# A graph layer with routed experts on one core: accumulating transfers listed by a new rule, in two batches, and node groups of two tiles at the end

## The chip, the core and the metric

The kernel is one program on one core of a Trainium2 chip. The metric is the device time of one execution in microseconds; a kernel's figure is the median of its runs. PE is the matrix engine, DVE the vector engine, ACT the scalar engine, POOL the GpSimd engine; SP only starts DMAs. Each engine works through its own instruction list in order and waits at semaphores.

## What is computed

```python
def reference(x, src, dst, ...):          # x: 6250 nodes x 256, 106250 edges
    x = x + relu(segment_sum(norm_src * (layernorm(x) @ W)[src], dst) * norm_dst + b)
    n = layernorm(x)                      # then a feed-forward of 8 experts
    top_p, top_idx = top_k(softmax(n @ Wr + br), 2)
    w = top_p / top_p.sum(-1)             # of 2 experts per node
    y_e = gelu(expert_norm_e(n) @ W1[e] + b1[e]) @ W2[e] + b2[e]   # 256 -> 1024 -> 256
    return x + w[0] * y_{e0} + w[1] * y_{e1}
```

Every node gathers the rows of its in-neighbours; then each node's row goes through two of eight experts, and both results are weighted and added to the node's row.

## The kernel before, in words

**Edges.** The edges are sorted by target and cut into 832 tiles of 128. A step `fetch` gathers 128 source rows by an indirect DMA of POOL (L832) into a ring of 23 buffers `gt`; a step `tile` multiplies them on PE with a one-hot matrix `S` (L1165). After eight tiles, `add` (L1534) adds the sum to `acc`, which holds all 49 node tiles of 128 nodes.

**Nodes.** The 49 node tiles form eight chunks (ending at tiles 10, 17, 24, 31, 36, 41, 45, 49), and each chunk is cut into groups of at most four tiles. When the last edge of a group is added, a group has these steps: `nd1` (degree norm, DVE), per tile `nT`, `nW`, `hh`, `xT`, `lg` (transpose, W, residual and statistics, transpose, router logits; PE, ACT, DVE), `nd2` (layernorm factors; for tiles from 10 on SP then stores the rows of `acc` to `out`), `lr` (logits) and `xr` (normed rows into `xrow`).

**Routing.** When a chunk's groups are done: `r1` (top 2), `r3` (counts by matmul on PE, L1222 and on), `r5` (slots `slI`, DVE, L1451), `xs` (two indirect DMAs of POOL per node tile scatter the rows to `xs` in DRAM, sorted by expert, L861), `r6` (which expert each block of 256 rows has, DVE). For the last chunk SP also writes eight blank blocks (`blanks`, L1002).

**Blocks.** 56 blocks of 256 routed rows; chunk 6 gives blocks 34 to 37, chunk 7 gives 38 to 55. For each block SP loads rows and weights (`ld`: L1024 rows, L1028 `w1b` 1 MB; `ld2`: L1034 `w2b` 1 MB). PE does `turn` (transpose, L1235), four `up` (L1251) and two `down` (L1266); ACT the gelu; DVE `low`, `split` and `y` (L1688). A block's first `up` needs its `low`; `down` needs its four `split`. The hidden tiles `h32` rotate through four buffers.

**Putting results together.** Blocks 0 to 33 are early: SP stores their results to `ys` (L991), and once all edge tiles are done a step `cg` per node tile (0 to 40) gathers two rows per node from there on POOL (L880), and `cc` (DVE, L1699 to L1706) weights and adds them into `acc`. The gathered rows rotate through ten buffers, so `cg` t waits for `cc` t-10. Tiles 0 to 9 are complete then and SP stores them to `out` (L987). Tiles 10 to 40 were stored before without their expert results; their `cc` makes the sum alone, and `sums` adds it to `out` by one accumulating DMA per batch of tiles (L900). Blocks 34 to 55 are late: their results are added straight to `out` by a `give`, two accumulating indirect DMAs (L891). Gives and batches may hit the same rows, so each waits on POOL until the one before has landed; the first also waits for all plain stores to `out` (`wait_last`). Late results rotate through three buffers `yb` and then eight in `gt`.

**What sets the order.** A planner (`plan`, run when the program is built) simulates clocks of the four engines with costs in us and writes one list of steps; each engine gets the steps that concern it in that order. The steps of DMAs started by SP come in the same list. `step_give` decides when a give or a batch may be listed: not before `s["chain"]` (the supposed landing of the one before) and not when POOL's clock is too far ahead. `step_job` lists steps of nodes, routing and gathers. `free` ignores POOL.

Of the kernel before, what the change touches and what calls it, by code (L numbers as in the profile page):

```python
# [6 lines left out]
N, D, E, H = 6250, 256, 8, 1024  # L7
# [19 lines left out]
ENDS = [10, 17, 24, 31, 36, 41, 45, 49]  # L27
STEP = 4
CHUNKS = list(zip([0] + ENDS, ENDS))
PARTS_OF = [-(-(t1 - t0) // STEP) for t0, t1 in CHUNKS]  # L30
GROUPS = [(c, t0 + (t1 - t0) * i // k, t0 + (t1 - t0) * (i + 1) // k)
# [30 lines left out]
TG = CHUNKS[EARLY][1]  # L62

TP = 10
NSUM = -(-(TG - TP) // 11)
SUMS = [(TP + (TG - TP) * i // NSUM, TP + (TG - TP) * (i + 1) // NSUM) for i in range(NSUM)]
NA = NB - M0
# [99 lines left out]
def plan():  # L167

    order = []
    clock = {"PE": 0.0, "DVE": 0.0, "ACT": 0.0, "POOL": 0.0}  # L170
# [8 lines left out]
    def emit(kind, arg, costs, ready):  # L179
        order.append((kind, arg))  # L180
        t = ready
        for eng, us in costs:
            t = max(t, clock[eng]) + us
            clock[eng] = t
            t += 0.2
        return t + HAND
# [102 lines left out]
    gives = collections.deque()  # L289

    batches = collections.deque()

    def step_give():

        if max(s["chain"], s["plain"], s["base"]) > s["now"] or clock["POOL"] > s["now"] + 2.6:
            return False
        if batches and batches[0][0] <= s["now"]:
            b = batches.popleft()[1]
            emit("sums", b, (("POOL", 1.3 * (SUMS[b][1] - SUMS[b][0])),), s["now"])
            s["summed"] += 1  # L300
        elif gives:
            emit("give", gives.popleft(), (("POOL", 3.4),), s["now"])
            s["given"] += 1
        else:
            return False
        s["chain"] = clock["POOL"] + 5.0
        return True
# [32 lines left out]
    def step_job(front):  # L340
# [4 lines left out]
        for job in list(itertools.islice(front, 2 if front is jobs or front is sends else 1)):  # L345
            job.over()
            for chain in job.heads():
                if not chain.steps:
                    continue
                kind, arg, costs = chain.steps[0]  # L350
                if chain.at > s["now"] or not free(costs):
                    continue
                if kind == "cg" and clock["POOL"] > s["now"] + 2.5:
                    continue
# [49 lines left out]
                if kind == "routed":  # L404
                    s["routed"] = arg
                chain.at = end + 2.0 if kind == "cg" else s["now"] if kind == "xs" else end
                job.at = max(job.at, end)
# [51 lines left out]
def gnn_ffn(nc, x, src, dst, W, b, Wr, br, ln_g, ln_b, W1, b1, W2, b2, out):  # L459
# [8 lines left out]
    with ctx:  # L468
# [61 lines left out]

        PW, PL, PR, PV = PS[7][:, 0:256], PS[7][:, 256:256 + STEP * E], PS[7][:, 288:384], PS[7][:, 384:512]

# [1204 lines left out]
```

How the kernel before makes its waits and increments, by code:

```python
        def pool(e):  # L747
            def made(inst):
                inst.then_inc(s_const, 1)
            def count(tile, pattern, base=0, mult=0):
                made(e.iota(tile, pattern=pattern, base=base, channel_multiplier=mult, allow_small_or_imprecise_dtypes=True))
            made(e.memset(ident[:, :], 0.0))
            e.wait_ge(s_const, const["ident0"])
            made(e.affine_select(out=ident[:, :], in_=ident[:, :], compare_op=ALU.not_equal,
                                 fill=1.0, base=0, pattern=[[-1, 128]], channel_multiplier=1))
            count(irep[:, :, :], [[1, 128], [0, TC]])
            made(e.memset(ones[:, :], 1.0))
            made(e.memset(oneb[:, :], 1.0))
            e.wait_ge(s_const, const["oneb"])
            made(e.affine_select(out=tri[:, :], in_=oneb[:, :], compare_op=ALU.is_gt,
                                 fill=0.0, base=0, pattern=[[1, 128]], channel_multiplier=-1))
            count(irun[:, :, :], [[1, 128], [0, CT]])
            count(area[:, :], [[AREA, E]])
            count(room[:, :], [[AREA * BS, E]])
            count(gone[:, :], [[AREA, E]])
            count(rev[:, :], [[-1, E]], base=E)
            count(kio[:, :], [[1, MB]])
            count(pio[:, :], [[0, 1]], mult=1)
            e.wait_ge(s_const, const["pio"])
            for g in range(NGR - 1):
                inst = e.tensor_scalar(tardy[:, g:g + 1], pio[0:R, :], float(AFTER[g]), None, ALU.is_ge)
                if g == NGR - 2:
```

## Time and profile before

| | |
|---|---|
| median of 3 runs | 1668.92 us |
| the runs | 1669.75, 1660.30, 1668.92 us |
| profiled execution, its time | 1661.44 us |
| profiled execution, its span | 1660.0 us |
| mean granted PE clock | 0.82 |
| PE, POOL, DVE, ACT busy | 1192.6, 1116.0, 952.5, 595.0 us |
| chain that ended last: PE, DMA, POOL | 35%, 25%, 19% of the span |
| fetches (L832) on POOL | 832 of 1.0 us, 133 to 1338 us of the span |
| gives (L891) on POOL | 44 issues, 1394.7 to 1652.7 us |

A span runs from the first to the last instruction; the time of the execution holds what lies around it too. The chain is followed back from the last instruction to what released it. In the rows of a timeline the bracket at the end is how long the engine stood before this instruction and what ended that; in the rows of the chain of waits there is a start, a duration and what was under way, and a DMA there is the stretch from issue to landing.

### The profile page before, as it was taken

What the parts mean: (1) busy time and instruction counts of PE and PEld (TensorE: products, weight loads), DVE (VectorE), ACT (ScalarE), POOL (GpSimd) and SP (SyncE); (2) the same over time, 40 slices, a digit from 0 to 9 for tenths busy, and PEclk for the clock granted to TensorE, in tenths of its full rate; (3) what the DMA queues carried; (4) which work ended last, traced back from release to release, by engine and by line L of the source; (5) the groups of instructions that cost most, each with busy time, mean ns of one, the idle gap of its engine ahead of it and who ended that gap; (6) DMA issues with size and microseconds to landing.
All of it is one profiled execution on the core that took longest, in us unless ns stands there. A gap on an engine that the chain in (4) does not pass through costs nothing.

```text
span 1660.0 us, 26618 instructions
## 1 busy us (share of the span) xinstructions
PE 1192.6 (72%) x9098; PEld 989.6 (60%) x9098; DVE 952.5 (57%) x2502; ACT 595.0 (36%) x1169; POOL 1116.0 (67%) x1115
## 2 busy tenths in 40 slices
PE   6954565647358645995599659969839858689995
PEld 5954344535146314982488439848728747479984
DVE  8997456656434353656264734764645749466552
ACT  4954011111032004440345025516315335356662
POOL 5006777777777777777777777777777757673333
PEclk9999566666578557996699769979959969799998
DMA  6027866675375447974787469759658578999882
GB/s 187 1 98 266 266 219 203 213 232 179 117 260 163 110 119 261 312 222 129 260 270 253 138 217 316 255 192 305 188 189 292 179 252 265 258 294 305 264 251 51
DMA packets 195546, 354.75 MB, mean 214 GB/s; under 512 B 25572, under 2 KB 93446, under 8 KB 195412
## 3 DMA queue, kind: packets, MB, share of 16 engines
q1 hardware_dynamic: 130120, 205.39, 36.6%
q0 software_dynamic: 58928, 141.26, 29.5%
q10 hardware_dynamic: 6364, 6.40, 1.2%
q8 instruction: 73, 1.20, 0.3%
q14 instruction: 61, 0.50, 0.1%
HBM read 290.80 MB, written 64.07 MB: 214 GB/s over the span
## 4 chain that ended last, share of the span: by engine, by line
PE 35%; DMA 25%; POOL 19%; issue 9%; DVE 8%; ACT 3%; SPq 0%; POOLq 0%; DVEq 0%; ACTq 0%
DMA gt<-zt,srcI 12%; POOL gt L832 9%; PE ps L1251 9%; PE ps L1266 9%; PE ps L1165 8%; DMA out<-gt,toks 6%; POOL xs L861 6%; DMA out<-acc 3%; PE ps L1140 2%; POOL out L891 2%; PE ps L1176 2%; DVE ohl L1340 2%; PE ps L1203 2%; DMA xb<-xs 1%; ACT h L1112 1%
## 5 line engine op out<-in xcount | busy, mean ns | idle before, releaser
L832 POOL DMA_INDIRECT gt<-zt,srcI x832 | 834.1, 1003 | 254.2 <-issue 181.6
L1165 PE MATMUL ps<-gt,S 128*128 128x257 f16 x1664 | 345.7, 331 | 200.3 <-DMA gt<-zt,srcI 198.9
L1165 PEld LDWEIGHTS ps<-gt,S 128*128 128x128 f16 x1664 | 203.5, 152 | 298.2 <-DMA gt<-zt,srcI 282.8
L1251 PE MATMUL ps<-xe,w1b 128*128 128x256 f16 x2688 | 343.2, 282 | 36.0 <-DVE xe L1656 18.9
L1266 PE MATMUL ps<-w2b,hT 128*128 128x256 f16 x2688 | 315.5, 275 | 13.5 <-DVE yb L1688 7.7
L1251 PEld LDWEIGHTS ps<-xe,w1b 128*128 128x128 f16 x2688 | 269.9, 101 | 78.6 <-DVE xe L1656 21.6
L1112 ACT ACTIVATE h<-ps,cb 128x256 f32<-128x256 f32 x448 | 227.1, 557 | 241.4 <-PE ps L1251 236.4
L1662 DVE SCALAR_TENSOR_TENSOR hT<-h,cb,hT 128x512 f16<-128x512 f32 x224 | 167.7, 750 | 237.4 <-ACT hT L1116 236.8
L1266 PEld LDWEIGHTS ps<-w2b,hT 128*128 128x128 f16 x2688 | 264.3, 99 | 47.5 <-issue 15.4
L1116 ACT ACTIVATE hT<-h,cb 128x512 f16<-128x512 f32 x224 | 161.7, 722 | 7.3
L1090 ACT ACTIVATE aT<-ps 128x256 f32<-128x256 f32 x98 | 37.4, 381 | 314.7 <-PE ps L1196 314.6
L1388 DVE TENSOR_TENSOR S<-dlo,S 128x1024 f16<-128x1024 f16 x104 | 71.6, 689 | 102.4 <-PE ps L1165 101.7
L891 POOL DMA_INDIRECT out<-gt,toks x38 | 60.1, 1581 | 92.9 <-DMA out<-gt,toks 64.4
L1100 ACT ACTIVATE xe<-ps 128x512 f16<-128x512 f32 x56 | 32.5, 580 | 244.6 <-PE ps L1235 244.6
L861 POOL DMA_INDIRECT xs<-xrow,slI x98 | 98.4, 1004 | 29.9 <-issue 29.9
L1235 PE MATMUL ps<-ident,xb 128*128 128x128 f32 x224 | 37.9, 296 | 104.0 <-DMA xb<-xs 104.0
L1656 DVE SCALAR_TENSOR_TENSOR xe<-ps,xe 128x512 f16<-128x512 f32 x56 | 38.3, 683 | 120.5 <-ACT xe L1100 120.5
L1534 DVE SCALAR_TENSOR_TENSOR acc<-ps,dhi,acc 128x257 f32 x208 | 91.1, 479 | 22.8 <-PE ps L1165 8.8
L1235 PEld LDWEIGHTS ps<-ident,xb 128*128 128x128 f32 x224 | 28.3, 152 | 107.5 <-DMA xb<-xs 106.7
L1140 PE MATMUL ps<-ohh,ohl 128*128 128x49 bf16 x832 | 84.3, 278 | 9.7 <-DVE ohh L1341 8.9
L1140 PEld LDWEIGHTS ps<-ohh,ohl 128*128 128x128 bf16 x832 | 81.5, 150 | 12.8 <-DVE ohh L1341 12.8
L1176 PE MATMUL ps<-gb,w1b 128*128 128x1 f32 x256 | 52.4, 339 | 34.5 <-DMA w1b<-in_L_ffn_W 34.5
(264 smaller groups left out, 1246.7 us busy)
## 6 DMA issues: line engine op xcount, KB each, us to landing
w1b<-ws SPq DMA_DIRECT2D x56, 1024.0 KB, 6.5
w2b<-ws SPq DMA_DIRECT2D x56, 1024.0 KB, 8.1
ws<-w2b SPq DMA_DIRECT2D x16, 1024.0 KB, 5.0
xb<-xs SPq DMA_DIRECT2D x56, 260.0 KB, 8.3
gt<-zt,srcI POOLq DMA_INDIRECT x832, 4.2
ys<-yb SPq DMA_DIRECT2D x34, 256.0 KB, 7.8
w1b<-in_L_ffn_W SPq DMA_DIRECT2D x8, 1024.0 KB, 8.7
hT<-in_L_ffn_W SPq DMA_DIRECT2D x8, 1024.0 KB, 13.9
```

The source lines that it names most:

```text
L832: e.indirect_dma_start(out=gt[:, i % NG, :], out_offset=None, in_=zt, in_offset=bass.IndirectOffsetOnAxis(ap=srcI[:, c, r:r + 1].bitcast(u ...
L861: e.indirect_dma_start(out=xs, out_offset=bass.IndirectOffsetOnAxis(ap=slI[:, i, CHUNKS[c][0] + j:CHUNKS[c][0] + j + 1].bitcast(u32), axis=0),
L891: e.indirect_dma_start(out=out, out_offset=bass.IndirectOffsetOnAxis(ap=toks[:, a, i:i + 1].bitcast(u32), axis=0), in_=late_rows(a)[:, i, ...
L1112: inst = e.activation(h32[n % NH][:, z, :], UP[n % 2][:, z * BS:(z + 1) * BS], ACT.Gelu, bias=cb[m % 3][:, 2 * q + z:2 * q + z + 1], scale ...
L1116: e.activation(hT[m % 2][:, 0, 2 * q:2 * q + 2, :], h32[n % NH][:, :, :], ACT.Copy, scale=cb[m % 3][:, 9:10]).then_inc(s_hi, 1)
L1140: inst = e.matmul(PS[6][:, 0:T], ohl[c % 2][:, :, j], ohh[c % 2][:, :, j], start=(c == 0 and j == 0), stop=(c == NCH - 1 and j == TC - 1))
L1165: inst = e.matmul(PS[r % 2][:, 0:257], S[:, r % NS, :, c], gt[:, i % NG, part * 257:part * 257 + 257], start=(c == 0 and part == 0), stop= ...
L1176: inst = e.matmul(PV[:, j:j + 1], w3[:, kk, j * 128:(j + 1) * 128], gb[:, ex, 2 + kk:3 + kk], start=(kk == 0), stop=(kk == 1))
L1251: inst = e.matmul(UP[n % 2][:, z * BS:(z + 1) * BS], w[:, l, kk, j * 128:(j + 1) * 128], xe[m % 2][:, k, kk, :], start=(kk == 0 and l == 0 ...
L1266: inst = e.matmul(PY[:, h * D:(h + 1) * D], hT[m % 2][:, k, j, h * 128:(h + 1) * 128], w[:, l, j, :], start=(j == 0 and l == 0 and k == 0) ...
L1534: inst = e.scalar_tensor_tensor(out=a, in0=PS[r % 2][:, 0:257], scalar=dhi[:, w, r:r + 1], in1=a, op0=ALU.mult, op1=ALU.add)
L1662: e.scalar_tensor_tensor(out=hT[m % 2][:, 1, 2 * q:2 * q + 2, :], in0=h32[n % NH][:, :, :], scalar=cb[m % 3][:, 9:10], in1=hT[m % 2][:, 0, ...
```

## The change

It has four parts. (1) The last two chunks (tiles 41 to 48) are cut into groups of two tiles in place of four. (2) The sums of tiles 10 to 40 go to `out` in two batches (15 and 16 tiles) in place of three (10, 10, 11). (3) The planner's rule for gives and batches: they are listed only when POOL's clock is at most 0.5 us ahead (was 2.6 us), a give is taken as 3.7 us of POOL and landed 4.5 us later (was 3.4 and 5.0), a batch as 2.0 us of POOL and landed 3.0 + 1.1 us per tile later (was 1.3 us per tile of POOL and 5.0). (4) Gathers and scatters are listed only when POOL's clock is at most 0.3 us ahead, and not when the chain of gives comes free within about 1 us; a gather counts as landed 6.0 us after (was 2.0).

```diff
 ENDS = [10, 17, 24, 31, 36, 41, 45, 49]
-STEP = 4
 CHUNKS = list(zip([0] + ENDS, ENDS))
-PARTS_OF = [-(-(t1 - t0) // STEP) for t0, t1 in CHUNKS]
+
+STEPS = [4] * (len(ENDS) - 2) + [2, 2]
+PARTS_OF = [-(-(t1 - t0) // step) for (t0, t1), step in zip(CHUNKS, STEPS)]
...
-NSUM = -(-(TG - TP) // 11)
+NSUM = 2
...
-        if max(s["chain"], s["plain"], s["base"]) > s["now"] or clock["POOL"] > s["now"] + 2.6:
+        if max(s["chain"], s["plain"], s["base"]) > s["now"] or clock["POOL"] > s["now"] + 0.5:
             return False
         if batches and batches[0][0] <= s["now"]:
             b = batches.popleft()[1]
-            emit("sums", b, (("POOL", 1.3 * (SUMS[b][1] - SUMS[b][0])),), s["now"])
+            emit("sums", b, (("POOL", 2.0),), s["now"])
+            s["chain"] = clock["POOL"] + 3.0 + 1.1 * (SUMS[b][1] - SUMS[b][0])
             s["summed"] += 1
         elif gives:
-            emit("give", gives.popleft(), (("POOL", 3.4),), s["now"])
+            emit("give", gives.popleft(), (("POOL", 3.7),), s["now"])
+            s["chain"] = clock["POOL"] + 4.5
             s["given"] += 1
         else:
             return False
-        s["chain"] = clock["POOL"] + 5.0
         return True
...
-                if kind == "cg" and clock["POOL"] > s["now"] + 2.5:
+                if kind in ("cg", "xs") and (clock["POOL"] > s["now"] + 0.3 or (gives or batches) and s["now"] + 1.0 < max(s["chain"], s["plain"], s["base"]) + 1.0 < s["now"] + 2.0):
                     continue
...
-                chain.at = end + 2.0 if kind == "cg" else s["now"] if kind == "xs" else end
+                chain.at = end + 6.0 if kind == "cg" else s["now"] if kind == "xs" else end
```

POOL's list behind the gather of tile 13, before. `xrow`, `S` and `gt` are the buffers of a gather (two issues each), `xs` is the scatter of chunk 7, L891 a give, L900 a batch:

```order
L880 DMA gt<-ys,cidx 128x256 x6
L891 DMA out<-yb,toks 6250x256 x2
L880 DMA xrow<-ys,cidx 128x256 x6
L861 DMA xs<-xrow,slI 53504x260 x8
L891 DMA out<-yb,toks 6250x256 x2
L880 DMA S<-ys,cidx 128x256 x6
L900 DMA out<-acc 128x10x256
L880 DMA S<-ys,cidx 128x256 x2
L880 DMA gt<-ys,cidx 128x256 x4
L891 DMA out<-yb,toks 6250x256 x2
```

The same place now (lines are two higher):

```order
L882 DMA gt<-ys,cidx 128x256 x4
L863 DMA xs<-xrow,slI 53504x260 x8
L882 DMA gt<-ys,cidx 128x256 x2
L882 DMA xrow<-ys,cidx 128x256 x4
L893 DMA out<-yb,toks 6250x256 x2
L882 DMA xrow<-ys,cidx 128x256 x2
L882 DMA S<-ys,cidx 128x256 x2
L893 DMA out<-yb,toks 6250x256 x2
L882 DMA S<-ys,cidx 128x256 x4
L893 DMA out<-yb,toks 6250x256 x2
```

The scatter stood behind 17 gathers, a give and three more gathers; it stands behind 16 gathers now. From there on two gathers stand between gives, up to the give of block 38; the first batch (15 tiles) follows two gathers later, and the second one stands behind the give of block 42. POOL's whole order of the tail was: give 34, 35, batch 0, 36, 37, 38, batch 1, 39, 40, batch 2, 41 to 55; it is give 34 to 38, batch 0, 39 to 42, batch 1, 43 to 55.

SP's list behind the eight blank blocks, before (loads of blocks 38 and 39; the stores of tiles 7 to 9 stood ahead of the blank blocks):

```order
L1024 DMA xb<-xs 128x2x260
L1028 ISA
L1028 DMA w1b<-ws 128x4x1024
L1034 DMA w2b<-ws 128x4x1024
L1038 ISA
L1038 DMA b2b<-in_L_ffn_b 128x256
L1024 ISA
L1024 DMA xb<-xs 128x2x260
L1028 ISA
L1028 DMA w1b<-ws 128x4x1024
```

and now:

```order
L989 DMA out<-acc 128x256 x2
L1026 ISA
L1026 DMA xb<-xs 128x2x260
L1030 ISA
L1030 DMA w1b<-ws 128x4x1024
L1036 DMA w2b<-ws 128x4x1024
L1040 ISA
L1040 DMA b2b<-in_L_ffn_b 128x256
...
L1030 DMA w1b<-ws 128x4x1024
L989 DMA out<-acc 128x256
```

The stores of tiles 7 and 8 stand ahead of block 38's load, that of tile 9 behind block 39's.

DVE's list at the first blocks of chunk 7, before. L1705 and L1706 are one combining step, `xe` is a `low`, `hT` a `split`; the first combining step here is that of tile 21:

```order
L1652 COPY cb2<-cbt 128x12
L1705 TENSOR_SCALAR acc<-S,wts 128x256
L1706 SCALAR_TENSOR_TENSOR acc<-S,wts,acc 128x256
L1656 SCALAR_TENSOR_TENSOR xe0<-ps5,xe0 128x512
L1705 TENSOR_SCALAR acc<-S,wts 128x256
L1706 SCALAR_TENSOR_TENSOR acc<-S,wts,acc 128x256
L1648 TENSOR_LOAD ek7
L1648 ISA x2
L1652 ISA
L1652 COPY cb0<-cbt 128x12
L1662 SCALAR_TENSOR_TENSOR hT0<-h320,cb2,hT0 128x512
L1662 SCALAR_TENSOR_TENSOR hT0<-h321,cb2,hT0 128x512
```

and now, from the first `split` of block 38 on; the first combining step here is that of tile 19:

```order
L1664 SCALAR_TENSOR_TENSOR hT0<-h320,cb2,hT0 128x512
L1664 SCALAR_TENSOR_TENSOR hT0<-h321,cb2,hT0 128x512
L1707 TENSOR_SCALAR acc<-xrow,wts 128x256
L1708 SCALAR_TENSOR_TENSOR acc<-xrow,wts,acc 128x256
L1664 SCALAR_TENSOR_TENSOR hT0<-h322,cb2,hT0 128x512
L1658 SCALAR_TENSOR_TENSOR xe1<-ps5,xe1 128x512
L1707 TENSOR_SCALAR acc<-S,wts 128x256
L1708 SCALAR_TENSOR_TENSOR acc<-S,wts,acc 128x256
L1664 SCALAR_TENSOR_TENSOR hT0<-h323,cb2,hT0 128x512
L1664 SCALAR_TENSOR_TENSOR hT1<-h320,cb0,hT1 128x512
```

Where the combining steps of tiles 21 and 22 stood around the `low` of block 38, that of tile 19 now stands between two `split` steps of block 38 and ahead of the `low` of block 39.

## Rows read from the trace of the kernel before

**Rows 1.** The page: busy time, share of the span, instructions, by engine.

```profile
PE 1192.6 (72%) x9098; PEld 989.6 (60%) x9098; DVE 952.5 (57%) x2502; ACT 595.0 (36%) x1169; POOL 1116.0 (67%) x1115
```

**Rows 2.** Windows: stretch, length, busy per engine, PE clock, DMA share, GB/s.

```profile
1444.00:1480.00 36.00, 34.32 (x313) 30.35 (x311) 20.89 (x50) 23.68 (x43) 28.50 (x24) 1.00 1.02 326
...
1534.00:1600.00 66.00, 66.00 (x607) 59.40 (x606) 34.09 (x79) 43.86 (x81) 24.75 (x16) 1.00 0.85 258
```

**Rows 3.** Chain of waits, 1200 to 1660 us: start, duration, what.

```profile
1384.37 9.38 DMA out<-acc
...
1428.55 14.97 DMA out<-acc
...
1480.22 12.14 DMA out<-acc
...
1506.73 8.72 DMA out<-gt,toks
...
1516.30 17.46 DMA out<-acc
...
1536.67 6.71 DMA out<-gt,toks
```

**Rows 4.** Timeline of POOL: start, duration, instruction, idle before.

```profile
1348.94 0.94 POOL L880 DMA_INDIRECT S<-ys,cidx  x1 [11.19 <-DMA ys<-yb]
1350.19 0.95 POOL L880 DMA_INDIRECT S<-ys,cidx  x1 [0.30 <-issue]
...
1394.66 1.62 POOL L891 DMA_INDIRECT out<-yb,toks  x1 [1.94 <-DMA out<-acc]
...
1406.31 1.17 POOL L861 DMA_INDIRECT xs<-xrow,slI  x1 [0.31 <-issue]
...
1444.49 1.63 POOL L891 DMA_INDIRECT out<-yb,toks  x1 [6.45 <-DMA out<-acc]
...
1534.60 1.78 POOL L891 DMA_INDIRECT out<-gt,toks  x1 [16.30 <-DMA out<-acc]
...
1631.70 1.56 POOL L891 DMA_INDIRECT out<-gt,toks  x1 [5.67 <-DMA out<-gt,toks]
...
1638.28 1.56 POOL L891 DMA_INDIRECT out<-gt,toks  x1 [3.15 <-DMA out<-gt,toks]
...
1643.74 1.55 POOL L891 DMA_INDIRECT out<-gt,toks  x1 [2.04 <-DVE gt L1694]
...
1649.29 1.55 POOL L891 DMA_INDIRECT out<-gt,toks  x1 [2.14 <-DMA out<-gt,toks]
```

**Rows 5.** Timeline of PE.

```profile
1344.13 0.65 PE L1165 MATMUL ps<-gt,S 128*128 128x257 f16 x2 [2.18 <-DMA gt<-zt,srcI]
...
1389.84 0.24 PE L1222 MATMUL ps<-Mb,oneb 128*128 128x8 bf16 x4
...
1422.21 1.12 PE L1235 MATMUL ps<-ident,xb 128*128 128x128 f32 x4 [5.43 <-DMA xb<-xs]
...
1442.60 2.58 PE L1251 MATMUL ps<-xe,w1b 128*128 128x256 f16 x22 [1.55 <-DVE xe L1656]
```

**Rows 6.** Timeline of DVE.

```profile
1397.13 0.52 DVE L1451 CAST slI<-slF 128x8 int32<-128x8 f32 x1
...
1407.72 0.75 DVE L1688 SCALAR_TENSOR_TENSOR yb<-ps,cb,b2b 128x512 f32<-128x512 f32 x1
...
1429.22 0.55 DVE L1705 TENSOR_SCALAR acc<-S,wts 128x256 f32<-128x256 f32 x1 [10.70 <-DMA S<-ys,cidx]
...
1642.35 0.62 DVE L1694 TENSOR_SCALAR gt<-gt,gate 128x256 f32<-128x256 f32 x2
```

**Rows 7.** Timeline of SP: DMAs that it starts.

```profile
1397.22 9.60 SPq L1002 DMA_DIRECT2D xs<-blank  x8
...
1418.68 0.40 SPq L1024 DMA_DIRECT2D xb<-xs  x1
...
1623.97 0.37 SPq L1034 DMA_DIRECT2D w2b<-ws  x1
```

More of the change, by code:

```diff
@@ L529, in gnn_ffn @@
         PY, PX, PA = PS[4], PS[5], PS[6]
-        PW, PL, PR, PV = PS[7][:, 0:256], PS[7][:, 256:256 + STEP * E], PS[7][:, 288:384], PS[7][:, 384:512]
+        PW, PL, PR, PV = PS[7][:, 0:256], PS[7][:, 256:256 + max(STEPS) * E], PS[7][:, 288:384], PS[7][:, 384:512]
         ph = ExitStack()
```

## The prediction

> **What bounds the kernel now.** I read the page's sums first: PE is busy for 72% of the span, POOL for 67%, DVE for 57% [rows 1]. No engine is full, so the order of work decides, and the place of the change has to be read. The lists of steps are alike through most of the gathers of edges: PE's and DVE's up to chunk 6's first node group, POOL's up to ten fetches before chunk 6's scatter. So I went to the windows of the tail [rows 2]: from 1444 to 1480 and from 1534 to 1600 us the DMA engines' share is 1.02 and 0.85, and PE is busy 34.3 of 36 us and 66.0 of 66 us.
>
> The chain of waits from 1500 on [rows 3] is one alternation: a give (two indirect accumulating DMAs into `out`, L891), its landing, the next give. Gives 41 and 52 start at 1534.60 and 1631.70 [rows 4], 11 periods of 8.83 us. Three batches (L900) stand in the same chain with 14.97, 12.14 and 17.46 us of transfer [rows 3], about 0.95 us more until the next give begins (1444.49 - 1428.55 - 14.97) [rows 3, 4]. The last give starts at 1649.29, 10.7 us before the span's end. The other bound is near: the last block's `y` ends at 1642.97 (1642.35 + 0.62) [rows 6], so PE and DVE have only 6.3 us to spare.
>
> If the chain had been tight from its first give at 1394.66, 18 periods of 8.83, three of the short ones at the end (6.6, 5.5, 5.5) and 47.4 for the batches would have ended at 1618: it has some 31 us of slack. The slack lies between 1394 and 1534, where three gather steps (2.5 us each, two issues, one every 1.25 [rows 4]), a scatter of 8 issues and PE's late blocks stand between gives. Block 38, the first of the last 18, waits for the last chunk's routing: `r3` at 1389.84 [rows 5], slots at 1397.65 [rows 6], the scatter only at 1406.31 because POOL had a give and three gather steps first [rows 4], the load at 1418.68 [rows 7], its turn at 1422.21 [rows 5].
>
> **The change, term by term.**
> 1. *Groups of two tiles.* Two more nd1, nd2 and lr steps are small DVE work beside fetches. What counts is what PE does between the last tile (its matmuls end at 1344.8) and `r3` of chunk 7, so far 45.0 us [rows 5]. Four `up` steps (12 matmuls each, 66.0 us / 607 [rows 2], 1.31 us), one turn and two tiles' node work leave this stretch: about 10 us of busy work, plus part of its waits, as block 34 now runs under the last fetches. I take 13 us earlier, 1377, between 10 (only the busy work) and 16. Slots follow `r3` by 7.8 us: 1385.
> 2. *Scatter.* It moves in front of gather 16 and of all gives, so it starts with its slots, 21 us earlier, and ends near 1395.5. The load of block 38 also stands behind eight blank stores (9.60 us from 1397.22, `r3` + 7.4 [rows 7]) and behind the stores of tiles 7 and 8. These need `y` of block 36, which began at `r3` + 17.9 [rows 6]: all three conditions meet at `r3` + 21 to 22, so 1399. Block 38 begins 20 us earlier.
> 3. *What the first give waits for.* It needs the stores of tiles 0 to 9 landed. Tile 9's used to be issued before the blanks; now it stands on SP behind five loads of blocks 38 and 39, 3.4 MB (two of 260 KB, three of 1 MB). It is issued at about 1403. The old one took 9.38 us from its combining step [rows 3]; behind the loads I take 10, so the first give starts at **1413**, 18 us later than before, though POOL is free from 1404. Bounds: 1404 and 1420.
> 4. *Tight list from there.* Two gather steps are 5.0 us; a give is two issues of about 1.6 and two pickups of 0.3, 3.8 [rows 4]. Some 0.25 go to the slower first issue behind each, together 9.05 us, about the period of a tight give. Five such periods lead to the first batch at 1458. A batch costs 44.57 us for 31 tiles [rows 3], 1.44 a tile: 15 tiles 21.6 + 0.95, which also covers the eight gather steps inside (22.2). Give 39 at 1481, give 41 at 1499, the second batch at 1516.5, 16 tiles 23.0 + 0.95, give 43 at 1540.5. Nine periods of 8.83 make give 52 at 1620. The short periods began in the old run once the last weight load (issued 1623.97 [rows 7]) had landed; it comes some 7 us earlier, so I take 8 + 5.5 + 5.5: the last give at **1639**, 10 us earlier.
> 5. *PE.* Gather 19 now sits behind the first give and DVE's combining step 19 in front of a split of block 38. DVE works in order, so block 39's first `up` waits until 1413 + 3.8 + 2.5 + about 5 of landing + 1.5 = 1425.5, 17 us ahead of 1442.60 [rows 5]. The same head of line existed before: DVE stood 10.70 us for gather 20 [rows 6]. Nine combining steps then follow within some 26 us of block work, but their gathers need four and a half periods, 41 us, and 2 to 3 us of buffers hide little: 8 to 12 us are given back. The last `y` ends 5 to 9 us earlier, 1636. The ring of eight late rows stays open: `y` 51 would need give 43, landed by 1549, twenty us before it.
>
> The end is the later of 4 and 5, the chain by about 3 us: minus 10 us, 0.6%. One batch less saves only what in a batch doesn't grow with tiles. The three rows (10, 10, 11 tiles at 14.97, 12.14, 17.46) give no usable slope; nothing fixed is one bound, the shortest of them less ten gives' share nothing, so 0 to 4 us, and I take 0.
>
> A rule to weigh here: the Trainium skill, "DMA: Bandwidth & Descriptors", section "Anatomy of one DMA — SWDGE (gpsimd) path", fits a DMA as about 2.0 us plus its bytes over 436 GB/s. By it a batch of 1280 KB takes 5.0 us and the whole gain of the merge is 2.0 us; the trace disagrees about the size (12.14 to 17.46 us, accumulating beside loads), and the sum goes by the rows.
>
> **Rivals.**
> - *The stores don't hold the first give* (the loads in front pass quickly). Then it starts at 1404, chain and PE are both 9 us further ahead: minus 19 us, 1650. For it: 9.38 us was already measured beside traffic. Against it: five loads now stand directly ahead. On this the Trainium skill, same page, section "Queues, rings and completion order", says that each DMA engine consumes a sequencer's descriptors in ring order; by it the first give is at 1413 or later. The trace can't settle it, as no store stands behind loads there.
> - *The lead is lost in waits.* Step 5 gives back the whole 17 us because POOL waits inside each tight give with gathers queued behind it. The last `y` is back at 1643 and the last give near 1644: minus 5 to plus 5 us, 1664 to 1674. For it: DMA share already 1.02 in 1444 to 1480.
> - *Slower: landings grow.* The place is gives 34 to 52, 18 periods, now without slack and with block loads, gathers and a longer batch at once. Every us more of landing is 18 us. The longest landing in the chain is 8.72 against 6.71 in a usual one [rows 3]. With 2 us more in the mean: 36 - 10 = +26 us, 1695. It cancels the gain from 0.55 us on and costs 1% from 1.5 us on. Against it: from 1534 to 1600 the chain is tight already, with PE full and a share of 0.85.
> - *The edit does less than it says*: both batches still wait, and the scatter is held by slots rather than by POOL. That is contained in steps 2 and 4.
>
> **How the numbers follow.** The profiled execution took 1661.44 us, the median of three is 1668.92 (1660.30 to 1669.75), 7.5 us over it. Minus 10 makes 1651.4 for a profiled one and **1659 us** against the median. Chances: forecast (minus 5 to minus 15) 0.48; stores don't hold 0.22; lead lost 0.17; landings grow 0.13. Eight in ten: from 1644 (stores don't hold, plus a few us of the batch's and `r3`'s bounds) to 1680 (lead lost, with half a us on each landing). One per cent, 16.7 us, is about what a measurement of this kernel can tell from no change. Faster by more: most of the second case and a little of the first, 0.26. Slower by more: most of the last, 0.12. Within: 0.62.
>
> **What would show it.** `r3` of chunk 7 near 1377 and the scatter right after its slots: steps 1 and 2. POOL idle for about 9 us before the first give, released by a store to `out`: step 3; no idle means the second case. Gives at 9 us periods, a batch of 15 tiles near 22 us: step 4; a mean landing above 7.5 us means the slow case. DVE waiting for gathers 19 and 28 and PE behind it: step 5. The forecast is wrong if the last `y` ends after the last give could start, or if PE waits longer for block 34's load, whose turn now stands in front of tile 815.

## The result, and the profile after

The changed kernel takes 1670.24 us (median of 19 runs, 1664.75 to 1673.83), the kernel before 1662.85 us (19 runs, 1658.78 to 1670.04). The ratio is 1.0032, 95% interval [1.0021, 1.0044]: slower by 0.2 to 0.4%, where I forecast 0.6% faster. The ratio here and below comes from the single runs and need not be the quotient of the two medians; one of a_step4's twelve runs, of 2948 us, was a slow one and is left out of its ratio. The profiled execution took 1668.77 us with a span of 1667.3 us, 7.3 us longer than before. Lines of the changed kernel are two higher than before.

The page's busy times (the columns of [rows 1]) hardly move:

```profile
PE 1196.1 (72%) x9098; PEld 989.5 (59%) x9098; DVE 961.1 (58%) x2562; ACT 595.8 (36%) x1169; POOL 1120.6 (67%) x1116
```

The windows (the columns of [rows 2]; the second and third stretch are added) show where the work is missing:

```profile
1444.00:1480.00 36.00, 27.57 (x228) 23.22 (x225) 15.91 (x38) 17.96 (x32) 28.64 (x26) 0.90 1.02 260
1470.00:1495.00 25.00, 14.42 (x108) 11.69 (x106) 9.50 (x23) 7.74 (x15) 19.52 (x19) 0.73 1.09 259
1480.00:1494.00 14.00, 6.43 (x34) 4.71 (x35) 8.15 (x21) 0.00 (x0) 11.04 (x10) 0.52 1.02 294
1534.00:1600.00 66.00, 65.06 (x597) 58.36 (x596) 33.16 (x77) 42.79 (x78) 15.98 (x10) 1.00 0.95 267
```

From 1444 to 1480 PE is busy 27.6 us where it was 34.3 [rows 2]. From 1470 to 1495 it was busy 20.2 us before:

```profile
1470.00:1495.00 25.00, 20.22 (x172) 17.16 (x171) 14.54 (x36) 11.65 (x22) 17.52 (x16) 0.93 1.08 265
```

Timeline of POOL (start, duration, instruction, idle time before it and what ended it), the rows that answer to [rows 4]:

```profile
1389.35 1.02 POOL L863 DMA_INDIRECT xs<-xrow,slI  x1 [0.30 <-issue]
...
1418.57 1.62 POOL L893 DMA_INDIRECT out<-yb,toks  x1 [11.12 <-DMA out<-acc]
...
1465.19 2.34 POOL L902 DMA_DIRECT2D out<-acc  x1
1467.84 1.08 POOL L882 DMA_INDIRECT xrow<-ys,cidx  x1 [0.30 <-issue]
...
1488.74 1.84 POOL L893 DMA_INDIRECT out<-gt,toks  x1 [0.30 <-issue]
...
1509.18 1.67 POOL L893 DMA_INDIRECT out<-gt,toks  x1 [2.18 <-DMA out<-gt,toks]
...
1529.56 2.18 POOL L902 DMA_DIRECT2D out<-acc  x1 [6.18 <-issue]
...
1556.08 1.66 POOL L893 DMA_INDIRECT out<-gt,toks  x1 [24.34 <-DVE gt L1696]
...
1640.07 1.56 POOL L893 DMA_INDIRECT out<-gt,toks  x1 [7.34 <-DMA out<-gt,toks]
...
1657.52 1.56 POOL L893 DMA_INDIRECT out<-gt,toks  x1 [2.13 <-DMA out<-gt,toks]
```

The scatter is 17 us earlier than before, and the first give 24 us later. It stood 11.1 us for a store of `acc`. (Give 43, at 1556.08, has an instruction of a later `y` in its bracket. That one ended at the same moment; by the chain of waits below the give waited for the second batch, which landed at 1555.2.) By give 41 (1509.18) the chain is 25 us ahead of before, but before had all three batches behind it by then, and here the second one is still to come. With it, give 52 (1640.07) and the last give (1657.52) are 8.4 and 8.2 us behind [rows 4].

SP's own DMAs, and the same stretch in the chain of waits, with the two other long pieces of that chain (start, duration, what was under way):

```profile
1386.40 10.00 SPq L1004 DMA_DIRECT2D xs<-blank  x8
...
1401.85 0.40 SPq L1026 DMA_DIRECT2D xb<-xs  x1
...
1405.17 3.46 SPq L989 DMA_DIRECT2D out<-acc  x1
```

```profile
1405.17 12.49 DMA out<-acc
...
1469.22 15.44 DMA xrow<-ys,cidx
...
1529.56 25.69 DMA out<-acc
```

The store of tile 9 starts behind the loads of blocks 38 and 39 and needs 12.49 us from issue to landing, where it took 9.38 before [rows 3]. But its place among the loads is not most of the first give's delay. The combining step of tile 9 itself ends later. Its last instruction on DVE, before:

```profile
1383.85 0.49 DVE L1706 SCALAR_TENSOR_TENSOR acc<-xrow,wts,acc 128x256 f32<-128x256 f32 x1
```

and now:

```profile
1398.25 0.49 DVE L1708 SCALAR_TENSOR_TENSOR acc<-xrow,wts,acc 128x256 f32<-128x256 f32 x1
```

Of the 23.9 us by which the first give is later, 14.4 are this step (1398.74 for 1384.34), 6.4 are the store's wait on SP until 1405.17, and 3.1 are its longer landing. DVE didn't stand still before the step: in its new list the steps `r5` and `r6` of chunk 7 (1382 to 1393 us) come first, and before they came after it.

The second batch (16 tiles) takes 25.69 us, where the one of 11 tiles took 17.46.

Timelines of PE (first fence) and DVE (second), answering to [rows 5] and [rows 6]:

```profile
1376.23 0.24 PE L1224 MATMUL ps<-Mb,oneb 128*128 128x8 bf16 x4
...
1405.58 0.66 PE L1237 MATMUL ps<-ident,xb 128*128 128x128 f32 x4 [1.94 <-DMA xb<-xs]
...
1431.39 0.82 PE L1253 MATMUL ps<-xe,w1b 128*128 128x256 f16 x3 [14.97 <-DVE xe L1658]
...
1487.57 5.28 PE L1268 MATMUL ps<-w2b,hT 128*128 128x256 f16 x24 [10.58 <-DVE gt L1690]
...
1494.29 0.60 PE L1237 MATMUL ps<-ident,xb 128*128 128x128 f32 x4
```

```profile
1429.19 0.35 DVE L1707 TENSOR_SCALAR acc<-xrow,wts 128x256 f32<-128x256 f32 x1 [13.45 <-DMA xrow<-ys,cidx]
...
1484.68 0.35 DVE L1707 TENSOR_SCALAR acc<-xrow,wts 128x256 f32<-128x256 f32 x1 [11.48 <-DMA xrow<-ys,cidx]
...
1648.61 0.75 DVE L1690 SCALAR_TENSOR_TENSOR gt<-ps,cb,b2b 128x512 f32<-128x512 f32 x1 [4.41 <-PE ps L1268]
```

Read the two together. DVE's combining step of tile 29 stands until 1484.68 for a gather that POOL started right behind the first batch; so block 40's `y` (1486.67) is late, the next `down` has to wait for it, and PE stands 10.6 us and then runs 24 matmuls in 5.28 us, where 24 take 2.78 us at full clock: the granted clock from 1480 to 1494 was 0.52, the lower of the two levels. That was not PE's only loss. Its lead over before was 16.6 us at the turn of block 38 (1405.58), 11.2 at block 39's first `up` (1431.39), and only 1.2 at the turn of block 42 (1469.84 for 1471.00), ahead of this stall: PE had stood for `low` steps behind late gathers, the last time 5.4 us until 1460.70, and ran until 1466 at a granted clock of 0.50. The stall behind the batch then costs 7.0 us more: the turn of block 43 starts at 1494.3, before it started at 1488.4. The last `y` ends at 1650.05 (its second part, 1649.39 + 0.66), 7.1 us later than before.

### The profile page after: what moved, and what is told of

Its sections match the earlier page's. It is cut to its first block, busy times and chain, and to the rows that moved or that the text cites. A ratio compares the mean times of both kernels' runs of the same rounds, so it can differ in the third digit from the quotient of the medians.

```text
span 1667.3 us, 26685 instructions
## 1 busy us (share of the span) xinstructions
PE 1196.1 (72%) x9098; PEld 989.5 (59%) x9098; DVE 961.1 (58%) x2562; ACT 595.8 (36%) x1169; POOL 1120.6 (67%) x1116
## 4 chain that ended last, share of the span: by engine, by line
PE 35%; DMA 26%; POOL 16%; DVE 10%; issue 9%; ACT 3%; DVEq 0%; POOLq 0%; SPq 0%; ACTq 0%
DMA gt<-zt,srcI 14%; PE ps L1167 9%; PE ps L1268 9%; PE ps L1253 8%; POOL gt L834 8%; DMA out<-gt,toks 5%; POOL xs L863 5%; PE ps L1178 3%; PE ps L1142 2%; DMA out<-acc 2%; POOL out L893 2%; DVE ohl L1342 2%; PE ps L1205 2%; ACT h L1114 1%; DVE zh L1356 1%
## 5 line engine op out<-in xcount | busy, mean ns | idle before, releaser
L1167 PE MATMUL ps<-gt,S 128*128 128x257 f16 x1664 | 347.5, 329 | 202.9 <-DMA gt<-zt,srcI 201.8
L1167 PEld LDWEIGHTS ps<-gt,S 128*128 128x128 f16 x1664 | 201.9, 151 | 304.3 <-DMA gt<-zt,srcI 290.4
L893 POOL DMA_INDIRECT out<-gt,toks x38 | 60.9, 1603 | 100.3 <-DMA out<-gt,toks 69.0
L1536 DVE SCALAR_TENSOR_TENSOR acc<-ps,dhi,acc 128x257 f32 x208 | 91.1, 479 | 23.8 <-PE ps L1167 9.2
```

What stands on the lines that cost most here:

```text
L893: e.indirect_dma_start(out=out, out_offset=bass.IndirectOffsetOnAxis(ap=toks[:, a, i:i + 1].bitcast(u32), axis=0), in_=late_rows(a)[:, i, ...
L1167: inst = e.matmul(PS[r % 2][:, 0:257], S[:, r % NS, :, c], gt[:, i % NG, part * 257:part * 257 + 257], start=(c == 0 and part == 0), stop= ...
L1536: inst = e.scalar_tensor_tensor(out=a, in0=PS[r % 2][:, 0:257], scalar=dhi[:, w, r:r + 1], in1=a, op0=ALU.mult, op1=ALU.add)
```

## Experiments

All ran on four other chips, on which both kernels are slower: 1918 to 1943 us for the kernel before, with the fetches of edges taking longest (last fetch at 1548 us in the trace of b_two below, 1337 us before). Each ratio is to the kernel before on the same chip, in the same call; the changed kernel has nearly the ratio there (1.0047, 1.004) that it has in the result (1.0032), so the change can be taken apart on them. Parts (3) and (4) of the change, the planner's rules, were always kept together; "the rule" below means both. Each kernel has one traced execution, which can lie several us off its median, so places in two traces are best compared from a point in the same trace. No trace of the kernel before was taken there; b_two stands for it.

| kernel | chip | us, median | before | ratio, 95% interval |
|---|---|---|---|---|
| after_again | B | 1933.80 | 1921.54 | 1.0047 [1.0023, 1.0071] |
| after_c | C | 1953.24 | 1943.50 | 1.0040 [1.0023, 1.0056] |
| b_groups: before, groups of two | A | 1943.67 | 1917.68 | 1.0127 [1.0091, 1.0163] |
| b_groups_c: the same | C | 1964.02 | 1943.50 | 1.0095 [1.0069, 1.0121] |
| b_two: before, two batches | A | 1920.54 | 1917.68 | 1.0020 [0.9995, 1.0044] |
| a_step4: after, groups of four | B | 1909.47 | 1921.54 | 0.9931 [0.9904, 0.9957] |
| a_step4_b: the same | C | 1929.31 | 1943.50 | 0.9921 [0.9900, 0.9942] |
| a_g7: after, groups of two in chunk 7 alone | C | 1926.85 | 1943.50 | 0.9907 [0.9887, 0.9928] |
| a_g7_2: the same | D | 1921.70 | 1940.26 | 0.9915 [0.9881, 0.9950] |
| a_g6: after, groups of two in chunk 6 alone | D | 1945.47 | 1940.26 | 1.0034 [1.0008, 1.0059] |
| a_store: after, tile 9's store ahead | A | 1916.24 | 1917.68 | 0.9983 [0.9955, 1.0012] |
| a_store_2: the same | B | 1920.95 | 1921.54 | 1.0003 [0.9977, 1.0028] |
| a_g7_late9: a_g7, tile 9's store behind the loads | D | 1935.61 | 1940.26 | 0.9983 [0.9964, 1.0003] |
| a_late: after, batches behind the last gather | A | 1939.41 | 1917.68 | 1.0103 [1.0060, 1.0146] |
| b_late2: b_two, batches behind the last gather | B | 1939.00 | 1921.54 | 1.0083 [1.0052, 1.0114] |
| a_g7_three: a_g7, three batches | D | 1929.36 | 1940.26 | 0.9946 [0.9923, 0.9970] |

### The parts of the change: groups or rule

b_groups (and b_groups_c) puts the new groups into the kernel before; b_two puts the two batches there; a_step4 (and a_step4_b) takes the groups out of the changed kernel, which leaves the rule and the two batches:

```diff
# b_groups
-STEP = 4
+STEPS = [4] * (len(ENDS) - 2) + [2, 2]
# b_two
-NSUM = -(-(TG - TP) // 11)
+NSUM = 2
# a_step4
-STEPS = [4] * (len(ENDS) - 2) + [2, 2]
+STEPS = [4] * len(ENDS)
```

> The kernel before with the first part of the change alone: groups of two tiles in the last two chunks; three batches, old rule of the planner. The routing matmul of chunk 7 should come at about 1377 us and block 38's turn at about 1405, as in the changed kernel (1376.2, 1405.6). Theory S (the first give waits for the store of tile 9, which now stands behind the loads of blocks 38 and 39, and a late chain of gives is not caught up): first give at 1415 or later, time within 0.5% of before. Theory Q (gathers issued behind a batch land only with it, and the combining step holds DVE and so PE): the first batch again stands in front of gathers, PE's lead of 17 us shrinks by some 15 us at each batch that gathers follow, time 0 to -0.4%. If neither holds, the 17 us lead stays and the time is 0.7% below before.

> The kernel before with the second part alone: two batches of 15 and 16 tiles, old rule. Theory Q: the gather behind the first batch lands about 23 us after it (16 us before), DVE and PE stand 6 to 8 us longer there, but there is one batch fewer with gathers behind; last y within 5 us of 1642, time -0.3 to +0.4%. Theory S: the first give is as in the kernel before (1394.7), so the chain keeps its slack and the time is that of before, at best 3 us less for a batch saved.

> The changed kernel with groups of four tiles everywhere: the planner's new rule and two batches without the first part. The order puts the first give between scatters of chunk 7 and tile 9's store ahead of the blank blocks, so theory S gives a first give near 1395 to 1400 and a time at or below before's (ratio 0.994 to 1.000); block 38 starts where before's does. Theory Q: 14 gathers around one batch of 15 tiles, DVE stands 17 us or more once, last y 0 to 8 us later than before's, ratio 1.000 to 1.005. If the groups are what costs, the ratio is at most 1.000; if the rule costs, it is that of the changed kernel or more.

> The changed kernel with node groups of four tiles again, second time: the new rule and the two batches alone. Where the first give no longer waits behind tile 9's late store and tile 831 follows its fetch closely, the ratio to before is 0.990 to 0.996 (it was 0.9931 on one chip), on this chip too. If the gain there was chance, or hangs on that chip, the ratio is 0.998 to 1.004.

> The kernel before with groups of two tiles in the last two chunks and nothing else. Groups cost, the rest gains: ratio 1.008 to 1.016, the step of tile 9 and with it the first give later than in before. If the loss on the other chip came from its slow fetches (tile 831 22 us behind the last fetch), the ratio is 1.000 to 1.004 on a chip that fetches faster, and unchanged on one like it.

> The changed kernel itself, beside the others, so that they have it from the same chip: the first four kernels ran on a chip on which the kernel before takes 1917.7 us. On a chip like the first one: ratio to before 1.002 to 1.005, first give 24 us later than before's, last y 7 us later. On a chip like the second one: the tile after the last gather of edges comes late and the ratio is not known; if the change costs there what its groups alone cost (1.0127), it is 1.00 to 1.015.

> The changed kernel itself, as the third corner beside the two others of this call. Ratio to before 1.002 to 1.006. The theory that the groups of two cost and the rest gains puts it at least 0.7% above the kernel with groups of four; the theory that the cost is in the gathers queued behind the batches (which groups of four have too) puts it within 0.3% of that kernel.

Measured: groups of two alone cost 0.95 and 1.27%, more than the 0.5% that I allowed at most for b_groups. The rule with two batches gains 0.69 and 0.79%. Both together, on chip C, give plus 0.40%, where the product of the parts (1.0095 x 0.9921) is plus 0.15%, inside the parts' intervals. Two batches alone change nothing that these runs can tell. So the change holds a gain from the rule and a larger cost from the groups. That the gain is about as large as my 0.6% is luck: I had built mine on what the groups bring forward, and the rule gains its 0.7 to 0.8% without them.

### Which groups

The list of a_g7 (groups of two in the last chunk, 7) has one tile behind the turn of block 34, the lists of a_g6 and of the changed kernel have 17.

```diff
# a_g7, a_g7_2
-STEPS = [4] * (len(ENDS) - 2) + [2, 2]
+STEPS = [4] * (len(ENDS) - 1) + [2]
# a_g6
-STEPS = [4] * (len(ENDS) - 2) + [2, 2]
+STEPS = [4] * (len(ENDS) - 2) + [2, 4]
```

> The changed kernel with groups of two in the last chunk alone. Its list has only one tile behind the turn of block 34 (17 in the changed kernel, 4 in before), so PE isn't held in front of the last tiles, and r3 of chunk 7 stands two turns earlier than with groups of four. If the cost of groups is PE's wait in front of the last tiles and the late tile 9, this one is at 0.990 to 0.997 of before, as good as groups of four or better. If small groups cost by their combining work beside the gives, it is at 0.999 to 1.004.

> The same kernel with groups of two in the last chunk alone and two batches, second time, as the base of the two others. Ratio to before 0.989 to 0.993 if the first reading was no chance.

> The changed kernel with groups of two in chunk 6 alone (the one before the last); the last chunk has groups of four again. Its list has 17 tiles behind the turn of block 34, as the changed kernel. If the cost of groups is what PE does in front of the last tiles, and so the late step of tile 9, this one is as slow as the changed kernel: 1.002 to 1.008 of before, tile 831 over 18 us behind its fetch where fetches are slow. If either half of the groups costs by itself, it is at 0.996 to 1.001, between 0.99 and the changed kernel.

Measured on one chip: a_g6 1.0034, a_g7_2 0.9915, 23.8 us apart. The groups of chunk 6 carry the whole cost on these chips. Those of chunk 7 cost nothing and gain at most a little: on chip C a_g7 is at 0.9907 and a_step4_b at 0.9921, with intervals that overlap. a_g7 beats both kernels.

PE in a_g6, its last tile's matmuls (L1167) and `r3` of chunk 7:

```profile
1599.76 0.39 PE L1167 MATMUL ps<-gt,S 128*128 128x257 f16 x2
...
1658.04 0.25 PE L1224 MATMUL ps<-Mb,oneb 128*128 128x8 bf16 x4
```

and in a_g7_2:

```profile
1580.05 0.54 PE L1167 MATMUL ps<-gt,S 128*128 128x257 f16 x2
...
1624.48 0.24 PE L1224 MATMUL ps<-Mb,oneb 128*128 128x8 bf16 x4
```

The two traces overstate the difference: that of a_g6 is of the slowest of its ten runs (1952.82 us), that of a_g7_2 of the fastest of its five (1915.94 us). So the 15 us by which the last fetch (1579.05 and 1563.98) is later need not be the groups' alone. Counted inside each trace, three things stay:

| | a_g6 | a_g7_2 |
|---|---|---|
| the last hundred fetches, first start to last start | 199.2 us | 192.6 us |
| start of the last fetch to `r3` of chunk 7 | 79.0 us | 60.5 us |
| start of the last fetch to that of the last give | 362.4 us | 340.6 us |

The last hundred fetches take longer on chip B too: 194.3 us in after_again, 186.4 in a_step4. On chip D most of the cost lies behind the last fetch: 21.8 us there, 23.8 us in the medians. In the result's own traces the hundred fetches took 152.2 us where before took 151.1, and the last tile moved only from 1344.1 to 1345.2 us, so this part of the cost shows on the four chips alone.

I expected this of a_g7 too little: its last tile's matmuls end 15 to 17 us behind the start of the last fetch, 7 in a_step4_b, and it is fast all the same. So the distance from the last fetch to the last tile isn't what decides.

### The first give's wait

The planner's lists put tile 9's store behind the loads of blocks 38 and 39 only when both chunks have groups of two (the changed kernel, b_groups). With groups of four, with groups of two in chunk 7 alone and with groups of two in chunk 6 alone, it is ahead of them.

The SP loop of a_store walks its own copy of the list, with tile 9's store in front of block 38's load. The one of a_g7_late9 does the opposite to a_g7, in whose list that store is ahead by itself (the steps of tiles 10 to 12, which it moves too, start nothing on SP):

```diff
# a_store, a_store_2
-            for kind, arg in ORDER:
+            own = list(ORDER)
+            own.remove(("cc", 9))
+            own.insert(own.index(("ld", 38)), ("cc", 9))
+            for kind, arg in own:
# a_g7_late9, from a_g7
-            for kind, arg in ORDER:
+            own = [o for o in ORDER if o not in (("cc", 9), ("cc", 10), ("cc", 11), ("cc", 12))]
+            at = own.index(("ld", 39)) + 1
+            own[at:at] = [("cc", t) for t in range(9, 13)]
+            for kind, arg in own:
```

> The changed kernel with one store moved on SP alone: tile 9's rows are stored before block 38's load, not behind block 39's. Theory S: the first give starts at 1408 to 1411 in place of 1418.6, every later give and batch comes 7 to 10 us earlier, and the end too (ratio to before 0.997 to 1.000). Theory Q: PE still ends as late as in the changed kernel, minus what gather 19 comes earlier, so the last y gains 0 to 8 us. If the first give is not what sets the end, the time stays at 1.003.

> The changed kernel with tile 9's store ahead of block 38's load on SP, as before, now beside the changed kernel. Theory S: 6 to 10 us below the changed kernel, first give 7 to 10 us earlier. Theory Q alone: within 2 us of it.

> The kernel with groups of two in the last chunk alone, with the store of tile 9 moved on SP from in front of the loads of blocks 38 and 39 to behind them, and nothing else. It tests the first give's wait alone. If that wait costs what moving the store ahead gained (0.4 to 0.5%), the first give is 10 us or more later than in the kernel without the move and the ratio 0.995 to 0.997. If lead and lag of the first give are lost later anyway, it is 0.990 to 0.992, as without the move.

The first and the last give on POOL in after_again:

```profile
1678.51 1.63 POOL L893 DMA_INDIRECT out<-yb,toks  x1 [15.72 <-DMA out<-acc]
...
1921.26 1.56 POOL L893 DMA_INDIRECT out<-gt,toks  x1 [2.13 <-DMA out<-gt,toks]
```

in a_store_2, same chip:

```profile
1659.34 1.62 POOL L893 DMA_INDIRECT out<-yb,toks  x1 [2.32 <-DMA out<-acc]
...
1901.45 1.56 POOL L893 DMA_INDIRECT out<-gt,toks  x1 [2.13 <-DMA out<-gt,toks]
```

in a_g7_late9:

```profile
1682.08 1.62 POOL L893 DMA_INDIRECT out<-yb,toks  x1 [14.51 <-DMA out<-acc]
...
1924.67 1.55 POOL L893 DMA_INDIRECT out<-gt,toks  x1 [2.01 <-DVE gt L1699]
```

and in a_g7_2, same chip:

```profile
1664.24 1.83 POOL L893 DMA_INDIRECT out<-yb,toks  x1 [0.30 <-issue]
...
1904.57 1.55 POOL L893 DMA_INDIRECT out<-gt,toks  x1 [2.93 <-DVE gt L1696]
```

In both pairs only the place of one 128 KB store differs. The first give is 19.2 and 17.8 us later with the store behind the loads, but 5.9 and 3.1 us of this were there already at `r3` of chunk 7, which the store can't touch (1633.23 and 1627.35; 1627.62 and 1624.48). From `r3` on, the first give is 13.3 and 14.7 us later and the last one 13.9 and 17.0: 240 us further on nothing of it has been caught up. The medians say the same, 12.9 us (a_store_2 against after_again, intervals that just overlap) and 13.9 us (a_g7_late9 against a_g7_2, intervals apart). Tile 9's store behind the loads costs 0.4 to 0.7%. I had expected 6 to 10 us for the first pair and 0.995 to 0.997 for a_g7_late9, too little both times.

It is not the whole cost of the groups. a_store_2 is still 11.5 us slower than a_step4 on the same chip (1.0003 and 0.9931, intervals apart), though from the last fetch to the last give both take about the same (348.3 and 349.6 us). And a_g6 has its store ahead of the loads and is as slow as the changed kernel.

### The gathers behind a batch

The rival theory (Q in the expectations; S is the one of the first give's wait) took the wait at tile 29's combining step for the cause: gathers that POOL starts behind a batch land only with it. a_late and b_late2 list a batch only once the last gather is listed:

```diff
# a_late; b_late2 is the same in before, with NSUM = 2
-        if batches and batches[0][0] <= s["now"]:
+        if batches and batches[0][0] <= s["now"] and s["read_all"]:
...
+                if kind == "cg" and arg == TG - 1:
+                    s["read_all"] = True
```

> The changed kernel with one more condition: no batch is listed before the last gather, so that no gather stands behind a batch. Theory Q: the combining step of tile 29 no longer waits 17 us for its gather, the last y comes 10 us or more earlier than 1648.6, weight loads end earlier with it, more of the last gives are short, and the end comes 3 to 8 us before the changed kernel's. Theory S alone: first give again at 1418, 21 gives and two batches in series behind it, the same time as the changed kernel (ratio to before 1.003). If gathers are not what a batch delays, the last y stays near 1648.

> The kernel before (groups of four, old rule) with two batches that are listed only behind the last gather. Theory Q: no combining step waits more than some 10 us for its gather, PE is spared the stalls of 1428 to 1450 and 1480 to 1499, the last y comes 5 to 12 us earlier; the first give is where it was (1394.7 on the first chip), nine gives run in the slack, and the end comes 3 to 10 us before the kernel before. Theory S alone: the time of the kernel before, within 2 us, since its first give is not late. If a batch behind the gathers only lengthens the chain at its end, slower by up to 10 us.

DVE's combining step of tile 29 in after_again:

```profile
1748.61 0.35 DVE L1707 TENSOR_SCALAR acc<-xrow,wts 128x256 f32<-128x256 f32 x1 [17.71 <-DMA xrow<-ys,cidx]
```

the longest wait of a combining step in the same stretch in a_late (lines two higher again):

```profile
1735.70 0.44 DVE L1709 TENSOR_SCALAR acc<-xrow,wts 128x256 f32<-128x256 f32 x1 [5.03 <-DMA xrow<-ys,cidx]
```

and its batches, with the give behind them (43):

```profile
1780.84 2.32 POOL L904 DMA_DIRECT2D out<-acc  x1 [4.15 <-issue]
1807.13 2.13 POOL L904 DMA_DIRECT2D out<-acc  x1 [23.97 <-issue]
1834.20 1.66 POOL L895 DMA_INDIRECT out<-gt,toks  x1 [24.94 <-DMA out<-acc]
```

The long wait is gone, and from the turn of block 42 to that of 43 PE needs 11.3 us (1723.5 to 1734.8), 30.7 in after_again (1727.3 to 1758.0). So it is shown that a batch delays the gathers behind it. But PE doesn't keep the 19 us: in a_late it needs 25.7 us from the turn of 43 to that of 44 (11.5 in after_again), which DVE's waits for gathers there (5.03 us until 1735.70 and 0.92 us after it) don't account for. Counted from the last fetch the last `y` is only 1.9 us earlier. I can't say from this trace what that second stretch waits for, and the 10 us that I expected for PE didn't come.

a_late has the worse ratio (1.0103, on another chip), and b_late2 1.0083 where b_two has 1.0020: two batches in a row, landing 25.1 and 26.2 us after their starts, stand in the chain of gives behind the last gather, and give 43 starts 278.4 us after the last fetch where it started 259.0 us after it in after_again. Theory Q had given both a gain of 3 to 10 us.

As the cause of the slower time this theory falls for another reason: a_g7_2, 0.85% faster than before, has the same wait and the same stall. Its combining step waits

```profile
1725.94 0.56 DVE L1707 TENSOR_SCALAR acc<-xrow,wts 128x256 f32<-128x256 f32 x1 [16.06 <-DMA xrow<-ys,cidx]
```

and PE needs 31.1 us from the turn of block 41 to that of 42.

### The price of a batch

a_g7_three is a_g7 with `NSUM = 3`.

> The kernel with groups of two in the last chunk alone, but three batches of 10, 10 and 11 tiles. The prediction took a batch as costing by its tiles with nothing fixed: then the third batch costs only its 0.95 us behind the landing, 0 to 0.1%. With a fixed part of 4 us it is 0.2% slower than with two; if large batches hold the gathers behind them longest, it is up to 0.3% faster.

It is at 0.9946 [0.9923, 0.9970], a_g7_2 at 0.9915 [0.9881, 0.9950]. The intervals overlap: two batches are no worse, and a fixed part of 0 to 4 us stays as open as it was. The last of three, 11 tiles, started at 1766.91 and the give behind it at 1788.59, 21.7 us; that of 16 tiles in a_g7_2 took 22.7 us (1767.23 to 1789.90). But a batch of 16 tiles took anything from 22.0 us (a_g7_late9) to 28.0 us (a_store_2) over these kernels. A batch does not cost by its tiles alone, and no price per tile comes out of these runs.

## Why the prediction was wrong, point by point

Two steps failed. In the sum it is step 4: of the 18.5 us by which the last give came later than forecast (1657.5 for 1639), 13 are periods and batches that I took too short, and 5.6 are step 3. Among the parts of the change it is step 1, which counted the groups of two as a pure gain.

**Step 1, groups of two: priced with the wrong sign.** Its forecast was met: `r3` at 1376.2 (1377). But it counted only what PE is spared before `r3`, and priced the rest as small DVE work. Groups alone cost 0.95 to 1.27%, and those of chunk 6 carry it. What they move elsewhere in the list I didn't price. The combining step of tile 9 ends 14.4 us later in the result's own trace. On the other chips it ends 76.0 us behind the start of the last fetch in b_two, 86.7 in a_step4, 100.3 in after_again and 109.4 in b_groups, so the rule delays it some and the groups more. And with groups of two in both chunks tile 9's store stands behind the loads. I read that order in the changed list and never asked which part of the change makes it; with other groups the same rule leaves the store ahead, and the first give starts with no wait in a_g7_2. The store's place accounts for 0.4 to 0.7% on the other chips. What the rest of the cost is, the runs don't take apart: the last hundred fetches, 7 to 9 us longer there (table above; 193.6 us in b_groups, 184.6 in b_two), are in it.

**Step 2, scatter and block 38.** Scatter at 1389.35 (forecast right behind slots at 1385; slots came at 1383.3, POOL had gathers in front for 6 us). Turn of block 38 at 1405.6, 16.6 us earlier where I took 20: the eight blank stores (10.00 us) started at `r3` + 10.2, not + 7.4.

**Step 3, the first give.** The mechanism was right: 11.12 us of idle POOL, released by the store. Its size was 5.6 us short, 1418.6 for 1413: the store was issued at 1405.2 where I took 1403, needed 12.49 us to land where I took 10, and 0.9 us more went by until the give. It is within my bounds (1404 to 1420). (The five loads in front are 3.5 MB, not 3.4.) What I didn't see is that the late combining step by itself delays the first give: with the store issued right after it and landing in 9.38 us as before, the give could not have started before about 1409, an estimate from the rows above. So the 1404 of the first rival was out of reach. The Trainium skill, "DMA: Bandwidth & Descriptors", section "Queues, rings and completion order", has each DMA engine consume the descriptors of a ring in ring order; the pairs of the third experiment agree (13.3 and 14.7 us for one store moved past the loads).

**Step 4, the chain: the term of the sum that failed.** From the first give on nearly everything was dearer than I took it: five periods 46.6 us (45.2), first batch to give 39 23.5 (22.5), 39 to 41 20.4 (18.1), 41 to the second batch 20.4 (17.7), second batch to give 43 26.5 (24.0), nine periods to give 52 84.0 (79.5), the last three 17.4 (19). The sum is 13 us over mine; with step 3's 5.6 the last give is 18.5 us behind the forecast 1639. The whole periods of the old run are a poor base: 1534.60 to 1631.70 [rows 4] ran 8.83 us in the mean, and 9.33 here with the same mechanism. From 1534 to 1600 the DMA engines' share is 0.95 here and was 0.85 there [rows 2]; that this is why landings take longer is likely, but no run tests it. The rule that fits a DMA as 2.0 us plus bytes over 436 GB/s (the Trainium skill, same page, section "Anatomy of one DMA — SWDGE (gpsimd) path") would have the 16 tiles, 2 MB, landed in 6.8 us, an estimate by the page's figures. The trace disagrees: the chain shows 25.69.

**Step 5, PE.** Block 39's first `up` at 1431.4 (forecast 1425.5; its terms add up to 1425.8), 11 us ahead of before. I let 8 to 12 us be given back over the next combining steps, and up to the turn of block 42 it was 10.0: this term was right. What I left out is the stall behind the first batch, which takes 7.0 us more than before needed at this place; in it 24 matmuls run 2.5 us longer at the lower clock. With the 5.9 us of the late start and a last 1.1 us, the last `y` ends at 1650, 7.1 us later than before where I took 7 us earlier. I had watched the gathers behind a give (the wait of 10.70 us in [rows 6] is for such a one, started at 1421 to 1422, ahead of the batch) and not those behind a batch. This did not set the end: the last give starts 7.5 us after that `y`.

**The rivals.** "The stores don't hold" is refuted by the trace and by the two pairs of kernels. "The lead is lost in waits" is what PE shows: 16.6 us ahead at block 38, 7.0 behind at block 55. "Landings grow" is there at part of its size: the nine tight periods to give 52 are 0.5 us longer, just under the 0.55 us from which I said that the gain is gone, and the batches 1 to 2.6 us. It ended on the slower side with two of the rivals holding at once, which I had priced only one at a time.

**Why it came out at plus 0.3%.** The parts, on chips where they could be separated: the rule and two batches minus 0.7 to 0.8%, groups of two in chunk 6 plus 1.0 to 1.3%. That these are the parts on the result's own chip too is argued from the nearly equal ratio of the whole, not shown: there the groups didn't delay the last tile, and the rule with groups of four was not measured on it.

## What to carry to other kernels

A chain of transfers in which each waits for the one before keeps what its first link is late wherever it has no slack: the 13 to 15 us of one small store behind loads were all still there 240 us later. So find what the first link waits for, and when that was ready, before pricing the periods. When one edit feeds a planner, price what the edit moves elsewhere in the list, and split the edit by parts before judging it: here a gain of 0.8% was hidden under a cost of over 1%. Before blaming the stall that looks worst in a trace, look whether the fastest kernel has it too: PE's stall behind the first batch is in the changed kernel and in a_g7_2.

## What the runs showed of the hardware

- A gather started on POOL behind an accumulating batch lands about when the batch does: the batch started at 1465.19 and had landed by 1483.73, the gather started at 1467.84 (its second half at 1469.22) and was used from 1484.68 on. In a_late, with all gathers ahead of the batches, no combining step after 1720 us waited more than 5.1 us.
- Accumulating batches of one size took different times from their start to the next give's: ten tiles 11.8 us (b_groups_c) to 18.8 us (a_g7_three), sixteen tiles 22.0 us (a_g7_late9) to 28.0 us (a_store_2).
- The changed kernel took 1669 us in its trace on one chip and 1933 and 1952 us on two others; 220 and 235 of these 264 and 283 us lie before its last fetch (1338.8, 1559.0 and 1573.6 us).
